# Quantized weights written as fp8's smallest number: clip on VectorE, one product into fp8 on ScalarE

## What is computed

```python
def weight_quant(w):
    scale = 1.0 / clip(mean(abs(w)), 1e-5)
    return clip(round(w * scale), -1, 1) / scale      # -1, 0 or 1, times one number
h = bit_linear(layernorm(x), w1)                      # 1024 -> 4096
h = silu(depthwise_conv1d(h, conv_w, conv_b))         # 3 taps along the rows
y = bit_linear(h, w2)                                 # 4096 -> 1024
```

## Time and profile before

| what | us |
|---|---|
| median of 3 runs (1546.15 to 1547.73) | 1547.21 |
| the profiled execution | 1546.65 |
| its slowest core, core 2, first to last instruction | 1545.0 |
| the other cores | 1532.2 to 1544.3 |
| TensorE, VectorE, ScalarE, GpSimd busy on core 2 | 1240.5, 1096.4, 908.4, 771.6 |

### The profile page before, as it was taken

The page is one execution under the profiler, slowest core; times in us unless marked ns, Lnnn a source line. Parts: engine busy times, 40 slices in busy tenths (PEclk is TensorE's granted clock), DMA queues, the critical chain, the costliest instruction groups (busy, mean ns, idle before and its releaser), DMA issues. The chain is left out here.

```text
span 1545.0 us, 32324 instructions; the slowest of 8 cores (1532.2 to 1545.0 us)
## 1 busy us (share of the span) xinstructions
PE 1240.5 (80%) x10500; PEld 841.0 (54%) x10500; DVE 1096.4 (71%) x2130; ACT 908.4 (59%) x1335; POOL 771.6 (50%) x718
## 2 busy tenths in 40 slices
PE   1124655899999999999458886668899999998998
PEld 0013433566666666665247774455566666665644
DVE  4699797788788788773635555587787887877740
ACT  2446866677787877773123331566676766766641
POOL 1266189586686775676600344025363553633531
PEclk9976766999999999999779998798999999999999
DMA  8816444212222212115030001010111211111011
GB/s 276 285 55 218 163 164 177 62 42 56 70 69 56 56 62 51 42 56 150 25 86 3 3 3 56 28 55 18 66 69 70 83 39 72 56 42 42 28 55 55
DMA packets 40684, 118.38 MB, mean 77 GB/s; under 512 B 4388, under 2 KB 12740, under 8 KB 40520
## 3 DMA queue, kind: packets, MB, share of 16 engines
q1 hardware_dynamic: 29144, 107.10, 19.8%
q0 software_dynamic: 11376, 9.22, 3.8%
HBM read 97.17 MB, written 25.70 MB: 80 GB/s over the span
## 5 line engine op out<-in xcount | busy, mean ns | idle before, releaser
L822 PE MATMUL bank<-xqT,w1q 128*128 128x258 bf16 (+1 forms) x4352 | 583.6, 281 | 99.5 <-DVE y L1170 52.6
L822 PEld LDWEIGHTS bank<-xqT,w1q 128*128 128x128 fp8e4 x4352 | 427.7, 102 | 258.6 <-issue 119.2
L851 PE MATMUL bank<-w2q,q 128*128 128x512 fp8e4 x2112 | 531.5, 381 | 0.0
L1397 POOL TENSOR_TENSOR y<-y,Rb 128x1024 f32<-128x1024 f32 (+1 forms) x136 | 338.1, 2509 | 200.8 <-ACT Rb L1042 200.8
L1002 ACT ACTIVATE y<-bank,convbs,convws 128x256 f32<-128x256 f32 (+1 forms) x544 | 295.6, 553 | 166.8 <-PE bank L822 154.9
L1228 DVE SCALAR_TENSOR_TENSOR y<-bank,convws,y 128x256 f32<-128x256 f32 (+1 forms) x544 | 256.0, 471 | 193.3 <-ACT y L1002 192.0
L851 PEld LDWEIGHTS bank<-w2q,q 128*128 128x128 f16 x2112 | 205.0, 98 | 165.2 <-issue 6.3
L1170 DVE SCALAR_TENSOR_TENSOR y<-bank,convws,y 128x256 f32<-128x256 f32 (+1 forms) x544 | 253.5, 466 | 0.1
L939 ACT ACTIVATE y<-y 128x1024 f32<-128x1024 f32 (+1 forms) x136 | 140.0, 1029 | 115.3 <-DVE y L1170 113.4
L1111 DVE TENSOR_TENSOR M<-M,ab 128x1024 f32<-128x1024 f32 (+1 forms) x119 | 195.8, 1645 | 1.9 <-ACT ab L951 1.9
L961 ACT ACTIVATE q<-y,qoff 128x1024 f16<-128x1024 f32 (+1 forms) x136 | 151.2, 1114 | 22.9 <-POOL y L1397 12.9
(11 more groups left out here) (200 smaller groups left out, 1458.9 us busy)
## 6 DMA issues: line engine op xcount, KB each, us to landing
w2r<-w2T SPq DMA_DIRECT2D x28, 1024.0 KB, 6.7
w1r<-w1T SPq DMA_DIRECT2D x7, 2048.0 KB, 25.7
x1t<-xall SPq DMA_DIRECT2D x19, 512.0 KB, 3.6
basebuf<-x1t SPq DMA_DIRECT2D x17, 512.0 KB, 2.6
xg<-xall SPq DMA_DIRECT2D x16, 512.0 KB, 4.6
x1t<-x2buf SPq DMA_DIRECT2D x16, 512.0 KB, 3.6
out<-x1t SPq DMA_DIRECT2D x16, 512.0 KB, 2.6
xg<-basebuf SPq DMA_DIRECT2D x14, 512.0 KB, 4.2
```

The costliest lines, as they stand in the source:

```text
L822: mm = pe.matmul(a_bank(n)[:, 0:tw + 2], w1q[:, c, k * P:(k + 1) * P], xqT[j % 3][:, c, 0:tw + 2], start=c == 0, stop=c == DC - 1)
L851: pe.matmul(pB[e % 2][:], q[:, qs, kh, :], w2q[:, kh, 512 * h:512 * h + 512], start=kh == 0, stop=False)
L1397: pool.tensor_tensor(v, v, Rb[:, 0:w].unsqueeze(1).to_broadcast([P, 4, w]), ALU.mult).then_inc(scaled_done, 1)
```

## The change

The middle step goes. The piece is multiplied by `rwu` = `rw`·2^-9 and written straight into fp8. The smallest fp8 number here is 2^-9, so that the conversion rounds to -1, 0 or 1 times 2^-9; the factor 2^9 goes into `convws` and `m2h`. GpSimd no longer touches the weights, and its loop runs over all tiles. ScalarE puts 4 of the first 8 pieces of `w1` (before: none), 18 of the other 24 (before 9) and 24 of 32 of `w2` (as before); VectorE puts 4, 6 and 8 (before 8, 15, 8). VectorE sums 7 loads of `w2` instead of 3. The slot tables move: 10 clips ahead of tile 0 instead of 12, puts one slot after the clip or so instead of three, column sums from slot 26 in fours instead of from 24 in threes.

```diff
-    SCALE1 = ['act' if u < 8 and u % 2 else 'pool' for u in range(32)]
-    PUT1 = ['act' if u >= 8 and u % 5 in (0, 2) else 'dve' for u in range(32)]
-    CLIP1_AHEAD = 12
-    CLIP1_SLOT = {u: (u - 12) * 17 // 24 for u in range(12, 32)}
-    PUT1_SLOT = {u: (u - 8) * 17 // 24 + 3 for u in range(8, 32)}
+    PUT1 = ['act' if (u % 2 if u < 8 else u % 4) else 'dve' for u in range(32)]
+    CLIP1_AHEAD = 10
+    CLIP1_SLOT = {u: (u - 10) * 17 // 22 for u in range(CLIP1_AHEAD, 32)}
+    PUT1_SLOT = {u: (u - 8) * 17 // 24 + 1 for u in range(8, 32)}
...
         dve.reciprocal(rw[:, w:w + 1], mw[:, w:w + 1]).then_inc(part, 1)
+        dve.wait_ge(part, 3)
+        dve.tensor_scalar(rwu[:, w:w + 1], rw[:, w:w + 1], UNIT, None, ALU.mult).then_inc(part, 1)
...
-    def w1_scale_pool(u):
-        pool.wait_ge(clip1, u + 1)
-        pool.tensor_scalar(piece(u), piece(u), rw[:, 0:1], cmag[:], ALU.mult, ALU.add).then_inc(scale1_p, 1)
+    def w1_put_dve(u):
+        dve.wait_ge(clip1, u + 1)
+        dve.tensor_scalar(w1q_at(u), piece(u), rwu[:, 0:1], None, ALU.mult, saturate=False).then_inc(put1_d, 1)
+    def w1_put_act(u):
         act.wait_ge(clip1, u + 1)
-        act.activation(piece(u), piece(u), AF.Identity, bias=cmag[:], scale=rw[:, 0:1]).then_inc(scale1_a, 1)
+        act.activation(w1q_at(u), piece(u), AF.Identity, scale=rwu[:, 0:1], saturate=False).then_inc(put1_a, 1)
...
-    SUM2_SLOT = [2, 5, 7, 9, 11, 13, 15, 17, 18, 20, 22, 24, 26, 28, 30, 32]
-    SUM2_BY = ['dve' if i in (3, 8, 12) else 'act' for i in range(16)]
+    SUM2_SLOT = [3, 8, 9, 11, 12, 14, 16, 17, 19, 20, 22, 24, 25, 27, 29, 32]
+    SUM2_BY = ['dve' if i % 2 and i < 14 else 'act' for i in range(16)]
...
-    PUT2_SLOT = {u: min(31, CLIP2_SLOT[u] + 3) for u in range(32)}
+    PUT2_SLOT = {u: CLIP2_SLOT[u] + 1 for u in range(32)}
...
-    def w2_scale(u):
-        pool.wait_ge(clip2, u + 1)
-        pool.tensor_scalar(w2_piece(u), w2_piece(u), rw[:, 1:2], cmag[:], ALU.mult, ALU.add).then_inc(scale2, 1)
...
-                if ph == 1 and j == 1 and k >= 24:
+                if ph == 1 and j == 1 and k >= 26:
...
+            for u in range(0, 8, 2):
                 w1_clip(u)
-            for u in range(8):
+                w1_clip(u + 1)
                 w1_put_dve(u)
+            dve.wait_ge(cv_in, 16)
+            dve.tensor_scalar(convws[:], convwr[:], mw[:, 0:1], 1.0 / UNIT, ALU.mult, ALU.mult).then_inc(mean1, 1)
             for u in range(8, CLIP1_AHEAD):
                 w1_clip(u)
...
-        def window_0():
-        def window_1():
...
-        if ph == 1:
-            window_0()
-            window_1()
-        for j in range(2 if ph == 1 else 0, nt + 2):
+        for j in range(nt + 2):
```

More of the change, by code:

```diff
@@ L29 @@
 LN1E8 = 18.420680743952367
+UNIT = 2.0 ** -9
 XROWS = 2304
@@ L212, in build_nc @@
     cmag = small('cmag', 1)
-    nmag = small('nmag', 1)
+    rwu = small('rwu', 2)
     clp = small('clp', 4)
@@ L321, in build_nc @@
     clip1 = sem('clip1')
-    scale1_p = sem('scale1_p')
-    scale1_a = sem('scale1_a')
     put1_d = sem('put1_d')
@@ L331, in build_nc @@
     clip2 = sem('clip2')
-    scale2 = sem('scale2')
     put2_d = sem('put2_d')
@@ L392, in setup_dve @@
         dve.memset(cmag[:], MAGIC)
-        dve.memset(nmag[:], SHIFT)
         dve.memset(qoff[:], QOFF)
@@ L481, in w1_clip @@
         dve.tensor_scalar(piece(u), piece(u), clp[:, 0:1], clp[:, 1:2], ALU.min, ALU.max).then_inc(clip1, 1)
-    def w1_scale_pool(u):
-        pool.wait_ge(clip1, u + 1)
-        pool.tensor_scalar(piece(u), piece(u), rw[:, 0:1], cmag[:], ALU.mult, ALU.add).then_inc(scale1_p, 1)
-    def w1_scale_act(u):
-        act.wait_ge(clip1, u + 1)
-        act.activation(piece(u), piece(u), AF.Identity, bias=cmag[:], scale=rw[:, 0:1]).then_inc(scale1_a, 1)
[L491 to L503, removed]
+    def w1_put_dve(u):
+        dve.wait_ge(clip1, u + 1)
+        if u == 0:
+            dve.wait_ge(mean1, 4)
+        dve.tensor_scalar(w1q_at(u), piece(u), rwu[:, 0:1], None, ALU.mult, saturate=False).then_inc(put1_d, 1)
+    def w1_put_act(u):
+        act.wait_ge(clip1, u + 1)
+        act.activation(w1q_at(u), piece(u), AF.Identity, scale=rwu[:, 0:1], saturate=False).then_inc(put1_a, 1)
     def w1_ready(eng, u):
@@ L586, in w2_clip @@
         if u == 0:
-            dve.wait_ge(mean2, 3)
+            dve.wait_ge(mean2, 4)
         if u >= 8 and u % 2 == 0:
@@ L590, in w2_clip @@
         dve.tensor_scalar(w2_piece(u), w2_piece(u), clp[:, 2:3], clp[:, 3:4], ALU.min, ALU.max).then_inc(clip2, 1)
-    def w2_scale(u):
-        pool.wait_ge(clip2, u + 1)
-        pool.tensor_scalar(w2_piece(u), w2_piece(u), rw[:, 1:2], cmag[:], ALU.mult, ALU.add).then_inc(scale2, 1)
     def w2_put_dve(u):
-        dve.wait_ge(scale2, u + 1)
-        dve.tensor_scalar(w2q_at(u), w2_piece(u), SHIFT, None, ALU.add, saturate=False).then_inc(put2_d, 1)
+        dve.wait_ge(clip2, u + 1)
+        dve.tensor_scalar(w2q_at(u), w2_piece(u), rwu[:, 1:2], None, ALU.mult, saturate=False).then_inc(put2_d, 1)
     def w2_put_act(u):
-        act.wait_ge(scale2, u + 1)
-        act.activation(w2q_at(u), w2_piece(u), AF.Identity, bias=nmag[:], saturate=False).then_inc(put2_a, 1)
+        act.wait_ge(clip2, u + 1)
+        act.activation(w2q_at(u), w2_piece(u), AF.Identity, scale=rwu[:, 1:2], saturate=False).then_inc(put2_a, 1)
     NT = {1: NT1, 2: NT2}
@@ L828, in ffn_pe @@
                     pm_sem, pm_val = mean2, 2
-                if ph == 1 and j == 1 and k >= 24:
-                    if k == 24:
+                if ph == 1 and j == 1 and k >= 26:
+                    if k == 26:
                         pe.wait_ge(pm_sem, pm_val)
                         pe.wait_ge(xqT_done, n_p)
-                    for u in range(3 * (k - 24), 3 * (k - 24) + 3):
+                    for u in range(4 * (k - 26), 4 * (k - 26) + 4):
                         column_sums(u)
@@ L985, in ffn_act @@
                 w1_sum_act(i)
-            act.wait_ge(mean1, 3)
+            act.wait_ge(mean1, 4)
             for u in range(1, 8, 2):
-                w1_scale_act(u)
-            act.wait_ge(mean1, 4)
+                w1_put_act(u)
+            act.wait_ge(mean1, 5)
         for j in range(nt + 3):
@@ L1210, in ffn_dve @@
             w1_mean_dve()
-            for u in range(8):
+            for u in range(0, 8, 2):
                 w1_clip(u)
-            for u in range(8):
+                w1_clip(u + 1)
                 w1_put_dve(u)
+            dve.wait_ge(cv_in, 16)
+            dve.tensor_scalar(convws[:], convwr[:], mw[:, 0:1], 1.0 / UNIT, ALU.mult, ALU.mult).then_inc(mean1, 1)
             for u in range(8, CLIP1_AHEAD):
                 w1_clip(u)
-            dve.wait_ge(cv_in, 16)
-            dve.tensor_scalar(convws[:], convwr[:], mw[:, 0:1], None, ALU.mult).then_inc(mean1, 1)
-            dve.wait_ge(mean1, 4)
+            dve.wait_ge(mean1, 5)
         for j in range(nt + 3):
@@ L1293, in ffn_dve @@
                     mean_rest(1, mean2, mean2_mm)
-                    dve.tensor_scalar(m2h[:], mw[:, 1:2], 0.5, None, ALU.mult).then_inc(mean2, 1)
-                    dve.wait_ge(mean2, 4)
+                    dve.tensor_scalar(m2h[:], mw[:, 1:2], 0.5 / UNIT, None, ALU.mult).then_inc(mean2, 1)
+                    dve.wait_ge(mean2, 5)
                 if ph == 1 and j == 1:
```

## The result

The changed kernel takes 1529.22 us (median of 12 runs) against 1546.41 for the kernel before on the same chips; the ratio is 0.9895, 95% interval 0.9875 to 0.9915. Some executions of either kernel took 2% to 10% longer, with a lower TensorE clock on one half of the cores, so every ratio here compares only the others, and it can differ a little from the quotient of two medians. So it is faster, by 1.05%, and by half of what was forecast: 17 us, not 33.

The account below looks back on a forecast made before the run. Before 283.4 us a chain bounds stage A, VectorE is fullest in B, GpSimd with VectorE in C; afterwards TensorE is full. Gains 7.1 + 10.2 + 16.4 = 33.7 from 1546.65, plus 0.56, give 1513.5 us; 8-in-10 range 1499 to 1529.

Parts of the forecast that it names:

- What bounds the kernel: Whole kernel: TensorE is full from 283.4 us on, so whatever reaches slot 0 of tile 2 earlier ends equally earlier.
- Stage A: From the total for the mean of `w1` to the first tap: gain 7.1 us, bounds 5 and 8.
- Stage B: From the first tap to the total for the mean of `w2`: 82.2 us, gain 10.2, bounds 2.7 to 16.2.
- Stage C: From the total for the mean of `w2` to the first matmul with `w2q`: 81 us, gain 16.4, bounds 5.5 and 25.4.
- the first rival: ScalarE and VectorE get in each other's way through puts and taps: gain 13 to 19 us, 1528 to 1534; chance 0.09.
- The prediction's own sign: VectorE in B and C: idle time staying above 20 us would show the prediction wrong.
- what `scale_y` costs VectorE: In C, GpSimd's eight `scale_y` of 2.57 us each delay VectorE: 6 us taken, bounds 0 and 10.3.
- The prediction's rule of the Trainium skill: SBUF: GpSimd and a VectorE instruction streaming one tensor at double rate want the same port pair; time 1513.5 to 1528.
- The prediction's dearest case: In C, all eight `scale_y` hold VectorE for their whole length, 20.6 us: gain 19.2, 1528 us; chance 0.05.
- the second reading of `w2`: Rival in C: 12 loads of 1.05 MB become the bound, C 95 us, time about 1528; chance 0.04.
- the number's size: Rival on TensorE: smallest-fp8 operands make 6464 matmuls 5.2 ns dearer, cancelling 33.7 us; twice that gives 1581; slower: chance 0.03.
- the two rivals around 1528 to 1532: First: engines in each other's way, 1532, chance 0.09. Second: `scale_y` holds VectorE to its end in C, 1528, chance 0.05.

Follow-up runs that it names:

- later puts: Changed kernel with the puts of `w2` in tile 1 three slots behind the clips instead of one: ratio 0.9869 to the kernel before.
- clips first: Changed kernel with VectorE issuing a slot's clips in tile 1 before it waits for ScalarE's tap: 1517.12 us, ratio 0.9812 to the kernel before.

## Why the prediction was wrong

*What bounds the kernel* was right. The stages after slot 0 of tile 2 kept their length, and a shift there went through to the end.

*Stage A* was right, 6.8 for 7.1. The bound that counted was the first matmul group: 2 us where 1.25 was allowed, while VectorE was through about 1.2 us earlier than the sum said.

*Stage B* had its busy time right: 75.4 for the 76.2 of VectorE, and 69.5 for 70.3 of ScalarE. The idle time was 8.3 for 6. B came out at 83.8 for 82.2, which is 1.6 of the 2.4 us that its gain fell short; the other 0.8 is that the median core's B was 91.6 before and not core 2's 92.4.

*Stage C* is the step that failed, in two terms.

The larger is "Idle is 14.7 now ... The cause of the most of it, ScalarE's 25.4 us behind GpSimd, is gone; I take 5." It was 14.3. ScalarE's 25.4 us behind GpSimd were gone, but its put now waited for VectorE itself, 27.1 us, with the tap behind it. The prediction described this as the first rival, "Every put of ScalarE now waits for a clip made one or two slots earlier", and gave it 0.09, on the ground that both engines had over 10 us of slack. Slack over a stage says little of it: a put one slot behind its clip allows ScalarE to lead VectorE by about one slot, and VectorE needs ScalarE's lead for its taps. The experiments with later puts and with clips first put the price at 9.7 and 10.8 us, with VectorE as busy as before (79.9 and 79.7 us). The prediction's own sign for this came as well: VectorE's idle time in B and C is 22.6 us, above the 20 that it named.

The smaller is what `scale_y` costs VectorE: 6 us were taken, with 10.3 as the upper bound, half a length for each. Clips and puts lengthened by 11.5 us against the undisturbed durations, and taking `scale_y` nearly away gave 10.3 us of VectorE's busy time and 9.8 of C. So my upper bound was the value. What made it so is in the timeline: the `scale_y` come three in a row, and two clips in a row met one each, and over the stage six of the eight caught an instruction. The prediction's rule of the Trainium skill (page "SBUF — State Buffer", section "Who interferes with whom": the first to come keeps the port pair for its whole instruction) agrees with two clips that take 5.58 us beside 8.35 us of `scale_y`. The prediction's dearest case, 20.6 us lost in C, did not come; about half of it did.

Together 9.3 us more idle time (14.3 for 5) and 3.7 more busy time (79.7 for 76) make the 13 that C fell short (94 for 81 on core 1).

The other rivals: the second reading of `w2` caused no wait in C of the changed kernel. It did show when puts came three slots late (3.6 us), which is the price of that cure. TensorE took 282 and 382 ns with weights of 2^-9, 281 and 381 with weights of 1: the number's size costs nothing. The range ended at 1529.0. Of the two rivals around 1528 to 1532, the first had C's sum nearly right, 92 us from 10.3 for `scale_y` and 11.7 of idle time, where 9.8 and 14.3 came; but it gave B a gain of 2.7, and 7.8 came. The second was right in time by luck: it had 20.6 for `scale_y` and 5 of idle time. Each named one of the two causes. Their joint chance of 0.14 was too low, since the causes do not exclude each other.

## What to carry to other kernels

When a step between two engines is removed, its queue was also their slack: look at which instruction each now waits for, and at what stands behind it. With orders written by hand, put a producer's instruction ahead of the producer's own waits, or the consumer's two or three places later; here either was worth about 10 us of 94 for no change of work (the two together were not run). In the kernel before, where GpSimd was busy for 83.5 of 97.3 us, the same order was worth nothing. And when two engines exclude each other in SBUF, count the meetings by how the instructions lie in rows, not by mean busy shares.

## What the runs showed of the hardware

- A VectorE put with a pointer as factor, fp32 to fp8, takes 745 ns on average in stage B, between the one with a number (680 as the median over the kernel before) and the clip with two pointers (810). ScalarE's put with a pointer as scale takes 1145, as the one with a pointer as bias had (1147).
- GpSimd suffers from the meetings as well: its `scale_y` took 2794 ns on average in the changed kernel's C and 2574 in the old. In the old C four of the eight took 2342 to 2357 ns and four 2771 to 2842; in the changed kernel's C all eight took 2775 to 2846, and most of those of the later tiles 2352 to 2372.
- In the kernel before, VectorE's clips of `w2` grew by 0.2 us each, on average, when they were issued earlier, and the stage stayed as long as it was. A shorter wait in a list is no gain until the stage's marks move.
